# Reordering the ramp of a fused cross-attention and quantised FFN kernel

## Chip, cores and metric

The kernel runs on 1 core of a Trainium2 chip. The metric is device time in microseconds (us) of one execution. All times below come from one profiled execution of the kernel before, unless a median of runs is named.

## The reference

`x` is 4 x 2048 x 512 in fp32. It is first updated by an attention block and then by a feed-forward block.

```
attention: the mask leaves key j to query i only where j % 2048 == i; ctx has 154 rows
    row i < 154 : softmax over one unmasked key -> out row = ctx[i] @ Wv @ Wout + bout
    row i >= 154: all keys masked alike         -> out row = mean(ctx) @ Wv @ Wout + bout
x = x + out
h  = layernorm(layernorm(x)) * gamma + beta
hq = round(h * 127 / max|h|);  w1q = clip(round(w1 / mean|w1|), -1, 1)
g  = gelu(hq @ w1q.T * scales + b1)                      # 512 -> 2048
gq = round(g * 127 / max|g|);  w2q = clip(round(w2 / mean|w2|), -1, 1)
x  = x + gq @ w2q.T * scales + b2                        # 2048 -> 512
```

So the attention needs no softmax: it is the product Wv @ Wout applied to the context rows and to their mean, one set of rows for each of the 4 batches.

## The kernel before

The 8192 rows of x are cut into 64 tiles of 128 rows (`T`), rolled by two tiles, so that tiles 0 to 13 are rows of batch 0 which get only the mean row. Each engine runs one program whose order is written out by hand: SyncE (SP) issues loads, transposes and stores, ScalarE (ACT) and TensorE (PE), VectorE (DVE) and GpSimd (POOL) compute. Engines meet only through semaphores. A queue never steps past an instruction that waits.

**The ramp** (the lines ahead of the loops `for s in range(6, ...)`) does the work that happens once, beside the first six tiles:

- `context_mean` (L946, PE): the sum of the 154 rows of `ctx_b0` by a product with a tile of ones.
- `products` (L953, PE): Wv @ Wout, 32 fp32 products of 128x128 by 128x512, in 8 chunks `m` of the inner dimension (each waits for `wv` and `wout` of its chunk) and 4 quarters `k` of PSUM tile `p1`. It goes chunk by chunk, so all 4 quarters end together. Each product is two instructions of the trace.
- The mean row: DVE multiplies each chunk of Wv by the mean (`mean_product`, L669), ACT sums it (`mean_sum`, L497), DVE gathers (`mean_weighted`, L677), PE adds over partitions (`mean_row`, L963, after 14 of the 32 products), DVE adds the bias (`mean_row`, L688). POOL then adds this row to the tiles of x (`add_attention`, L323).
- w1 and w2: sum of absolute values (`abs_w1`, L503 and L728; `abs_w2`, L509), the total over partitions (`weight_total`, L967, PE, after 25 products), `weight_scale` (L740), rounding (`round_weights` L514, `round_w1` L747) and clipping (`clip`, L752).
- `copy_wvo` (L519, ACT) moves the product out of PSUM by quarters. `out_rows` (L974) and `tail_product` (L987) apply it to the context.
- b1: loaded four times over 32 partitions, split by POOL into three bf16 parts (`split_b1`, L316), and gathered by DVE into `b1rows` (`bias_rows`, L716).

**A tile t** passes: `add_attention` (POOL), `statistics` (DVE, L762), `inverse_std` (POOL, L337), `centre` (DVE, L768), `times_std` (ACT, L523), `add_beta` (POOL, L345), `x_scale` (DVE, L775), `round_x` (ACT, L528), `scale_rows` and `widen_x` (POOL, L357, L377), `transpose_x` (a DMA issued by SP, L214), `bias` (PE, L994) and `first_layer` (PE, L1007, two halves), `gelu` (ACT, L535, two halves), `half_scale`, `hidden_scale` (DVE, L787, L792), `round_h` (ACT, L544), `transpose_h` (DMA, L223), `widen_h` (DVE L803 and ACT L553, half each), `second_layer` (PE, L1017), `result` (DVE, L813), `store`. `bias(t)` writes over `p1`, so it waits for both `gelu` halves of tile t-1.

**Loads.** SP issues the context of batch 0, Wv, b1, w1 with x(1) to x(3) between, the context, x(4) to x(7). ACT issues Wout first, then x(0), bout, gamma, beta, then w2 in three goes; w2 pieces lie in buffers that other work frees (`load_w2_first` waits for `mean_done`, `load_w2_last` for `wvo_done`).

Of the kernel before, what the change touches and what calls it, by code (L numbers as in the profile page):

```python
# [33 lines left out]
def block_program(nc, x, ctxm_d, ctxt_d, wvT, wout_d, bout, w1T, b1, w2T, b2, gamma, beta, ctx_b0, out, tail_rows):  # L34
    es = ExitStack()
    with es:
# [6 lines left out]
        def sem(name):  # L43
# [55 lines left out]
        row_of = hT_words[:, P:P + 32]  # L99
        row_pick = hT_words[:, P + 32:P + 35]  # L100
        tail_out = wout[0:NB, 6, :]
        b1f = xq[:, :, :, :].rearrange("p a i n -> p (a i n)").bitcast(FP32)[:, 0:D]
        b1res = xqT[:, :, :, :, :].rearrange("p a i k n -> p (a i k n)").bitcast(FP32)[:, 0:2 * D]\
            .rearrange("p (a n) -> p a n", a=2)
        wv = hid[:, :, 0:HID].rearrange("p a (m n) -> p a m n", n=D)
        w2raw = [hqT[:, a, :, :, :].rearrange("p j e t -> p (j e t)").bitcast(FP32).rearrange("p (e n) -> p e n", e=2)
                 for a in range(2)]
        w2raw += [hq8[:, :, :].rearrange("p a n -> p (a n)").bitcast(FP32).rearrange("p (e n) -> p e n", e=2)]
        w2raw += [xr[:, 12:14, :], xr[:, 14:16, :]] + [wout[:, 2 * a:2 * a + 2, :] for a in range(3)]
# [13 lines left out]
        row_set, row_picked = sem("row_set"), sem("row_picked")  # L123
# [63 lines left out]
        def _(sp):  # L187
            def load_x(t):
                if t >= XS:
                    sp.wait_ge(y_stored[t % XS], 16 * (t // XS))  # L190
                sp.dma_start(xr[:, t % XS, :], x[t * P:(t + 1) * P, :]).then_inc(x_loaded[t % XS], 16)
# [4 lines left out]
            def load_w1(i):  # L196
                k, h = i // 2, i % 2
                sp.dma_start(raw1[:, k, h * HALF:(h + 1) * HALF], w1T[k * P:(k + 1) * P, h * HALF:(h + 1) * HALF])\
                    .then_inc(w1_loaded[i], 16)

# [30 lines left out]
            sp.dma_start(ctx_rows, ctx_b0[0:P, :]).then_inc(ctx_b0_loaded, 16)  # L231
            sp.dma_start(ctx_end, ctx_b0[P:KV, :]).then_inc(ctx_b0_loaded, 16)
            load_wv(0)
            for g in range(4):
                sp.dma_start(b1f[32 * g:32 * g + 32, :], b1[g * D:(g + 1) * D].partition_broadcast(32))\
                    .then_inc(b1_loaded, 16)
            for m in range(1, KI):
                load_wv(m)
            load_w1(0)
            load_w1(1)  # L240
            load_x(1)
            load_w1(2)
            load_x(2)
            load_w1(3)
            load_x(3)
            for i in range(4, 8):
                load_w1(i)
# [3 lines left out]
            for t in range(4, 8):  # L251
                load_x(t)
# [853 lines left out]
```

## Time and profile before

| | |
|---|---|
| median of 3 runs | 547.36 us (547.23 to 548.58) |
| time of the profiled execution | 546.68 us |
| its span (first to last instruction) | 545.0 us |
| busy: PE, DVE, ACT, POOL | 522.7, 451.2, 438.9, 404.7 us |
| idle time of PE in the span | 22.3 us |
| memory read, written | 34.08 MB, 17.00 MB |

The span is 1.7 us shorter than the time of its execution; the rest lies around the program. A busy time that stands near the span belongs to the engine that bounds the kernel on the average. Where in the span its idle time lies has to be read from the timeline.

### The profile page before, as it was taken

What the parts mean: (1) busy time and instruction counts of PE and PEld (TensorE: products, weight loads), DVE (VectorE), ACT (ScalarE), POOL (GpSimd) and SP (SyncE); (2) the same over time, 40 slices, a digit from 0 to 9 for tenths busy, and PEclk for the clock granted to TensorE, in tenths of its full rate; (3) what the DMA queues carried; (4) which work ended last, traced back from release to release, by engine and by line L of the source; (5) the groups of instructions that cost most, each with busy time, mean ns of one, the idle gap of its engine ahead of it and who ended that gap; (6) DMA issues with size and microseconds to landing.
All of it is one profiled execution on the core that took longest, in us unless ns stands there. A gap on an engine that the chain in (4) does not pass through costs nothing.

```text
span 545.0 us, 8050 instructions
## 1 busy us (share of the span) xinstructions
PE 522.7 (96%) x2371; PEld 224.9 (41%) x2418; DVE 451.2 (83%) x762; ACT 438.9 (81%) x444; POOL 404.7 (74%) x532
## 2 busy tenths in 40 slices
PE   6979887999999999999999999999999999999997
PEld 2433333444444444444444444444444444444443
DVE  1968998989998888888888888888888889887553
ACT  2557998968998888888888888888888888887762
POOL 2085795898998888888988888888888889873300
PEclk9988999999999999999999999999999999999999
DMA  9997226587554555455555555545555554434433
GB/s 285 397 395 227 90 43 156 114 232 179 137 140 128 121 127 134 129 141 140 133 126 125 120 141 139 126 123 121 122 139 132 140 141 102 99 67 102 101 78 97
DMA packets 136870, 78.88 MB, mean 145 GB/s; under 512 B 114037, under 2 KB 114037, under 8 KB 136827
## 3 DMA queue, kind: packets, MB, share of 16 engines
q1 hardware_dynamic: 133947, 71.03, 51.9%
q10 hardware_dynamic: 2880, 7.34, 3.8%
q8 instruction: 19, 0.31, 0.2%
q14 instruction: 24, 0.20, 0.1%
HBM read 34.08 MB, written 17.00 MB: 94 GB/s over the span
## 4 chain that ended last, share of the span: by engine, by line
PE 75%; issue 2%; ACT 2%; DMA 1%; SPq 1%; DVE 1%; POOL 0%; ACTq 0%; DVEq 0%; POOLq 0%
PE py L1028 37%; PE p L1013 36%; PE p L1003 3%; DMA hT<-hq 1%; DMA out<-xr 1%; ACT hid L541 1%; SPq L220 1%; ACT hq L550 0%; ACT hqT L559 0%; DVE xr L818 0%; SPq L228 0%; ACT xq L532 0%; DVE hmax L795 0%; DVE hid L789 0%; DVE xmax L777 0%
## 5 line engine op out<-in xcount | busy, mean ns | idle before, releaser
L1028 PE MATMUL py<-w2q,hqT 128*128 128x512 bf16 x1006 | 230.0, 379 | 3.8 <-DVE w2q L759 2.8
L1013 PE MATMUL p<-w1q,xqT 128*128 128x512 bf16 x995 | 229.0, 380 | 2.5 <-issue 1.4
L541 ACT ACTIVATE hid<-p,xdeq 128x1024 f32<-128x1024 f32 x128 | 141.7, 1108 | 26.8 <-PE p L1013 16.4
L550 ACT ACTIVATE hq<-hid,hscale 128x2048 int8<-128x2048 f32 x64 | 128.1, 2001 | 38.7 <-DVE hscale L801 38.7
L1028 PEld LDWEIGHTS py<-w2q,hqT 128*128 128x128 bf16 x1024 | 100.1, 98 | 123.9 <-issue 3.3
L1013 PEld LDWEIGHTS p<-w1q,xqT 128*128 128x128 bf16 x1024 | 95.0, 98 | 120.6 <-issue 14.9
L350 POOL TENSOR_TENSOR hx<-hx,beta_b 128x512 f32<-128x512 f32 x64 | 92.6, 1467 | 11.4 <-ACT hx L526 11.4
L795 DVE TENSOR_REDUCE hmax<-hid 128x1 f32<-128x1025 f32 x64 | 78.1, 1220 | 21.7 <-ACT hid L541 21.3
L335 POOL TENSOR_TENSOR xr<-xr,attn 128x512 f32<-128x512 f32 x64 | 81.8, 1295 | 18.0 <-DVE attn L691 13.3
L354 POOL TENSOR_TENSOR xr<-xr,b_b 128x512 f32<-128x512 f32 x64 | 92.4, 1462 | 0.0
L789 DVE TENSOR_REDUCE hid<-hid 128x1 f32<-128x1024 f32 x64 | 77.4, 1210 | 8.9 <-ACT hid L541 8.9
L809 DVE CAST hqT<-hT 128x1024 bf16<-128x1024 int8 x64 | 56.9, 889 | 27.7 <-PE py L1028 18.9
L559 ACT ACTIVATE hqT<-hT 128x1024 bf16<-128x1024 int8 x64 | 67.0, 1047 | 4.9 <-DMA hT<-hq 4.9
L381 POOL CAST xq<-xq 128x1024 bf16<-128x1024 int16 (+1 forms) x33 | 33.4, 1011 | 47.8 <-ACT xq L532 47.8
L772 DVE SCALAR_TENSOR_TENSOR hx<-xr,mv,gamma_b 128x512 f32<-128x512 f32 x64 | 53.4, 840 | 0.1
L818 DVE SCALAR_TENSOR_TENSOR xr<-py,hdeq,xr 128x512 f32<-128x512 f32 x64 | 47.4, 740 | 3.3 <-PE py L1028 3.3
L526 ACT ACTIVATE hx<-hx,rstd 128x512 f32<-128x512 f32 x64 | 42.8, 715 | 4.4 <-POOL rstd L342 2.6
L764 DVE BATCH_NORM_STATS2 stat<-xr 128x6 f32<-128x512 f32 x64 | 43.0, 672 | 0.6 <-POOL xr L335 0.6
L532 ACT ACTIVATE xq<-hx,xscale 128x512 int16<-128x512 f32 x64 | 42.7, 714 | 0.7 <-DVE xscale L784 0.7
L777 DVE TENSOR_REDUCE xmax<-hx 128x2 f32<-128x1024 f32 (+1 forms) x33 | 38.7, 1173 | 0.1
L385 POOL TENSOR_TENSOR hdeq<-hstep,wmean 128x1 f32<-128x1 f32 x64 | 25.5, 399 | 17.7 <-DVE hstep L798 17.7
L958 PE MATMUL p<-wout,hid 128*128 128x512 f32 x64 | 33.1, 679 | 0.0
(86 smaller groups left out, 290.9 us busy)
## 6 DMA issues: line engine op xcount, KB each, us to landing
out<-xr SPq DMA_DIRECT2D x64, 256.0 KB, 2.5
xr<-x SPq DMA_DIRECT2D x63, 256.0 KB, 2.9
raw<-w1T SPq DMA_DIRECT2D x8, 512.0 KB, 14.8
wout<-wout_d ACTq DMA_DIRECT2D x8, 256.0 KB, 7.1
hid<-wvT SPq DMA_DIRECT2D x8, 256.0 KB, 9.7
wout<-w2T ACTq DMA_DIRECT2D x3, 512.0 KB, 4.2
attn<-ctxm_d SPq DMA_DIRECT2D x4, 256.0 KB, 16.1
hqT<-w2T ACTq DMA_DIRECT2D x2, 512.0 KB, 7.8
```

Source lines behind the costliest of these rows:

```text
L335: pool.tensor_tensor(xtile(t, n), xtile(t, n), a, ALU.add).then_inc(x1_ready, n)
L350: pool.tensor_tensor(htile(t, n), htile(t, n), bb, ALU.add).then_inc(xnormed, n)
L354: pool.tensor_tensor(xtile(t), xtile(t), b2_b[:, :, :], ALU.add).then_inc(xb_ready, 1)
L541: nc.scalar.activation(hid[:, t % 2, h * HALF:(h + 1) * HALF], p1[:, h * HALF:(h + 1) * HALF], ACT.Gelu, scale=col(xdeq, t)).then_inc(gelu ...
L550: nc.scalar.activation(hq8[:, t % 2, :], hid[:, t % 2, 0:HID], ACT.Copy, scale=col(hscale, t))\
L559: nc.scalar.activation(hqT[:, t % 2, NJ // 2:, :, :], hT8[:, t % 2, HALF:].rearrange("p (j t e) -> p j e t", e=2, t=P), ACT.Copy).then_inc ...
L772: nc.vector.scalar_tensor_tensor(htile(t)[:, 0, :], xtile(t)[:, 0, :], mv[:, t % 8, 0:1], gamma_b[:, :], ALU.subtract, ALU.mult).then_inc( ...
L789: nc.vector.tensor_reduce(hid[:, t % 2, HID:HID + 1], hid[:, t % 2, 0:HALF], AX.X, ALU.max, apply_absolute_value=True).then_inc(hmax_half, 1)
L795: nc.vector.tensor_reduce(col(hmax, t), hid[:, t % 2, HALF:HID + 1], AX.X, ALU.max, apply_absolute_value=True).then_inc(hmax_done, 1)
L809: nc.vector.tensor_copy(hqT[:, t % 2, 0:NJ // 2, :, :], hT8[:, t % 2, 0:HALF].rearrange("p (j t e) -> p j e t", e=2, t=P))\
L1013: mm = nc.tensor.matmul(p1[:, n * D:(n + 1) * D], xT[:, k, :], w1q[:, k, n * D:(n + 1) * D], start=False, stop=(k == KD - 1))
L1028: mm = nc.tensor.matmul(py[:, t % 2, :], hqT[:, t % 2, c // 2, c % 2, :], w2q[:, c, :], start=(c == 0), stop=(c == 2 * NJ - 1))
```

## The change

Five things change, all of them in the ramp. The loops from tile 6 on stay as they are.

1. All loads but Wout go out on SP's queue, in a new order. w2 is issued by SP, two pieces ahead of the first `transpose_x` and six behind it. w2's pieces lie in other buffers. SP waits inside `load_x` for tiles 12 to 15.
2. `products` goes through quarters 0 and 1 of every chunk first, then through all chunks of quarter 2 and all of quarter 3. `weight_total(0)` stands after 30 products in place of 25. ACT's `copy_wvo` of each quarter is spread out between other work.
3. b1 is loaded once on 16 partitions, POOL splits it, SP stores the parts to memory and loads them back as `b1rows`. `bias_rows` of DVE and two selects of POOL go.
4. ACT starts with one small Gelu. PE starts with eight small products of ones by ones.
5. The written orders of SP, POOL, ACT, DVE and PE are rewritten. Among them: PE runs `out_rows` 1 and 2 ahead of the first layer of tile 0. POOL adds the mean row to four tiles ahead of the first `inverse_std`. `second_layer(0)` can begin on half of w2.

```diff
+            def load_w2(j):
+                if j == 3:
+                    sp.wait_ge(mean_done, 1)
+                if j == 5:
+                    sp.wait_ge(wvo_done, KD)
+                sp.dma_start(w2raw[j], w2T[j * 2 * P:(j + 1) * 2 * P, :].rearrange("(p e) n -> p e n", e=2))\
+                    .then_inc(w2_loaded[j], 16)
+            def store_b1():
+                sp.wait_ge(b1_split, 5)
...
+            def load_b1_rows():
+                sp.wait_ge(const_set, 4)
+                sp.wait_ge(b1_stored, 16)
+                for g in range(4):
+                    sp.dma_start(b1rows[32 * g:32 * g + 12, :], b1_pieces.rearrange("b a n -> (b a) n")[:, g * D:(g + 1) * D])\
+                        .then_inc(b1_rows, 16)
...
+            load_ctx_b0()
+            load_b1()
+            sp.dma_start(gamma_b[:, :], gamma.partition_broadcast(P)).then_inc(gamma_loaded, 16)
             load_wv(0)
...
+            load_wv(7)
+            load_x(0)
             load_w1(0)
             load_w1(1)
+            sp.dma_start(bout_b[:, :], bout.partition_broadcast(P)).then_inc(bout_loaded, 16)
             load_x(1)
+            load_x(2)
             load_w1(2)
             load_w1(3)
+            store_b1()
             load_x(3)
+            sp.dma_start(beta_b[:, :], beta.partition_broadcast(P)).then_inc(beta_loaded, 16)
+            load_w1(4)
+            load_w1(5)
+            load_x(4)
+            load_x(5)
+            load_x(6)
+            load_w1(6)
+            load_w1(7)
+            load_b1_rows()
+            load_w2(0)
+            load_ctx()
+            load_w2(1)
+            transpose_x(0)
+            load_w2(2)
...
+            load_w2(7)
+            load_x(7)
+            load_x(8)
+            load_x(9)
             sp.dma_start(b2_b[:, 0, :], b2.partition_broadcast(P)).then_inc(b2_loaded, 16)
+            load_x(10)
             transpose_x(1)
...
             pool.wait_ge(mean_copied, 1)
             add_attention(0, 1)
             add_attention(1, 1)
+            add_attention(2, 1)
+            add_attention(3, 1)
             pool.wait_ge(const_set, 3)
             inverse_std(0, 1)
+            inverse_std(1, 1)
...
+            def first_gelu():
+                act.wait_ge(const_set, 2)
+                nc.scalar.activation(wpart[:, 0, 6:8], neg_half[:, :], ACT.Gelu).then_inc(vmean_done, 1)
...
             abs_w1(1)
+            copy_wvo(0)
             abs_w1(2)
-            load_w2_first()
+            copy_wvo(1)
             abs_w1(3)
             times_std(0)
             abs_w1(5)
+            copy_wvo(2)
+            times_std(1)
             abs_w1(6)
             abs_w1(7)
-            times_std(1)
             round_x(0)
+            times_std(2)
+            times_std(3)
+            abs_w2(0)
+            copy_wvo(3)
             round_weights(0, 1)
             round_weights(0, 3)
...
+            def warm_up():
+                pe.wait_ge(const_set, 1)
+                for _ in range(8):
+                    nc.tensor.matmul(pa[:, 0:P], ones[:, :], ones[:, :], start=True, stop=True)
...
-                    m, k = i // KD, i % KD
-                    if k == 0:
+                    m, k = (i // 2, i % 2) if i < 2 * KI else (i % KI, i // KI)
+                    if i < 2 * KI and k == 0:
...
+            warm_up()
             context_mean()
             products(0, 14)
             mean_row()
-            products(14, 25)
+            products(14, 30)
             weight_total(0)
-            products(25, 32)
+            products(30, 32)
+            out_rows(0)
             bias(0)
-            out_rows(0)
+            out_rows(1)
+            out_rows(2)
             first_layer(0, 0)
             first_layer(0, 1)
-            out_rows(1)
-            tail_product()
             weight_total(1)
             bias(1)
             first_layer(1, 0)
             first_layer(1, 1)
-            out_rows(2)
+            out_rows(3)
             bias(2)
             first_layer(2, 0)
             first_layer(2, 1)
+            tail_product()
             bias(3)
             first_layer(3, 0)
             first_layer(3, 1)
-            out_rows(3)
             bias(4)
             first_layer(4, 0)
-            second_layer(0)
             first_layer(4, 1)
+            second_layer(0, 0, NJ)
+            second_layer(0, NJ)
             second_layer(1)
             bias(5)
             first_layer(5, 0)
+            second_layer(2)
             first_layer(5, 1)
-            second_layer(2)
```

In the cut parts ACT's new order goes on: `abs_w2(1)`, `times_std` 4 and 5, `round_x(1)`, `abs_w2` 2, 4, 3, 5, 6, 7, then the Gelu of tile 0 with `round_x` 2 and 3. DVE's new order between the scale of w1 and its rounding is: statistics(5), x_scale(1), three `ctx_sum`, centre(5), x_scale(2,2), `attn_rows(0)`, the fourth `ctx_sum`, `round_w1` 0 and 2, four clips, `attn_rows` 1 and 2, `weight_sum(1)`.

## Rows read from the trace of the kernel before

**Rows 1.** Timeline of PE: start, duration, line, operands, count, idle before and releaser.
```profile
5.31 2.04 PE L949 MATMUL py<-hx,hT 128*128 128x512 f32 x2 [5.31 <-DMA hx<-ctx_b]
...
9.28 14.17 PE L958 MATMUL p<-wout,hid 128*128 128x512 f32 x28
23.75 1.12 PE L965 MATMUL py<-xr,hT 128*128 128x512 f32 x2 [0.29 <-DVE xr L685]
24.71 9.61 PE L958 MATMUL p<-wout,hid 128*128 128x512 f32 x22
37.30 0.56 PE L970 MATMUL py<-wsum,hT 128*128 128x1 f32 x2 [2.98 <-DVE wsum L738]
37.72 9.29 PE L958 MATMUL p<-wout,hid 128*128 128x512 f32 x14
47.79 0.40 PE L1003 MATMUL p<-b1rows,xqT 32*128 32x512 bf16 x4 [0.78 <-ACT wvo L521]
48.11 3.70 PE L983 MATMUL pa<-wvo,attn 128*128 128x512 f32 x8
51.87 3.40 PE L1013 MATMUL p<-w1q,xqT 128*128 128x512 bf16 x15
```

**Rows 2.** The same view from 60 us to the end of the ramp.
```profile
63.56 0.35 PE L970 MATMUL py<-wsum,hT 128*128 128x1 f32 x2 [1.42 <-DVE wsum L738]
...
76.66 0.40 PE L1003 MATMUL p<-b1rows,xqT 32*128 32x512 bf16 x4 [1.54 <-ACT hid L541]
...
89.04 3.61 PE L1028 MATMUL py<-w2q,hqT 128*128 128x512 bf16 x16 [2.83 <-DVE w2q L759]
...
105.11 0.40 PE L1003 MATMUL p<-b1rows,xqT 32*128 32x512 bf16 x4
```

**Rows 3.** What PE waited for after 135 us: total, times, longest.
```profile
PE p L1013 <- issue: 1.3, 8, 0.2
```

**Rows 4.** Stretches: length, busy of PE, PEld, DVE, ACT, POOL (instructions), granted clock, DMA share, GB/s.
```profile
30.00:40.00 10.00, 7.02 (x16) 3.17 (x15) 6.74 (x16) 6.51 (x10) 8.62 (x11) 0.85 1.04 392
40.00:50.00 10.00, 9.22 (x21) 3.56 (x20) 7.25 (x12) 6.90 (x9) 4.27 (x8) 0.81 0.86 248
50.00:60.00 10.00, 9.95 (x32) 4.46 (x32) 9.74 (x18) 9.97 (x18) 8.23 (x12) 1.00 0.44 142
...
140.00:300.00 160.00, 158.89 (x772) 68.66 (x786) 141.06 (x243) 137.49 (x133) 138.87 (x177) 1.00 0.55 132
```

**Rows 5.** Timeline of ACT.
```profile
30.36 0.72 ACT L526 ACTIVATE hx<-hx,rstd 128x512 f32<-128x512 f32 x1 [2.60 <-POOL rstd L342]
...
35.73 1.06 ACT L506 ACTIVATE w1q<-raw 128x1024 bf16<-128x1024 f32 x1 [1.42 <-DMA raw<-w1T]
...
38.16 0.72 ACT L532 ACTIVATE xq<-hx,xscale 128x512 int16<-128x512 f32 x1 [0.67 <-DVE xscale L784]
...
44.47 0.60 ACT L521 ACTIVATE wvo<-p 128x512 f32<-128x512 f32 x1 [1.80 <-PE p L958]
...
57.40 1.28 ACT L541 ACT_TABLE_LOAD   x1
...
87.19 1.06 ACT L559 ACTIVATE hqT<-hT 128x1024 bf16<-128x1024 int8 x1 [2.63 <-DMA hT<-hq]
...
105.56 2.00 ACT L550 ACTIVATE hq<-hid,hscale 128x2048 int8<-128x2048 f32 x1
```

**Rows 6.** Timeline of DVE.
```profile
19.68 0.69 DVE L674 TENSOR_TENSOR hx<-hid,hx 128x512 f32<-128x512 f32 x1 [0.54 <-DMA hid<-wvT]
20.29 3.40 DVE L685 SCALAR_TENSOR_TENSOR xr<-wout,attn,xr 128x512 f32<-128x512 f32 x4
...
44.90 3.35 DVE L749 TENSOR_SCALAR w1q<-raw,wscale 128x2048 int16<-128x2048 f32 x2
48.17 3.56 DVE L759 TENSOR_SCALAR w1q<-w1q 128x2048 bf16<-128x2048 int16 x4
```

**Rows 7.** Timeline of POOL.
```profile
26.55 2.50 POOL L335 TENSOR_TENSOR xr<-xr,attn 128x512 f32<-128x512 f32 x2 [13.32 <-DVE attn L691]
```

**Rows 8.** Timeline of SP's queue.
```profile
41.58 15.98 SPq L220 DMA_TRANSPOSE xqT<-xq  x2
```

More of the change, by code:

```diff
@@ L31, with block_program @@
 QMAX = 127.0
-def block_program(nc, x, ctxm_d, ctxt_d, wvT, wout_d, bout, w1T, b1, w2T, b2, gamma, beta, ctx_b0, out, tail_rows):
+def block_program(nc, x, ctxm_d, ctxt_d, wvT, wout_d, bout, w1T, b1, w2T, b2, gamma, beta, ctx_b0, out, tail_rows, b1_pieces):
     es = ExitStack()
@@ L255, in _ @@
             transpose_x(1)
-            for t in range(8, 12):
-                load_x(t)
+            load_x(11)
+            load_x(12)
+            load_x(13)
             transpose_x(2)
@@ L269, in _ @@
             sp.dma_start(tail_rows, tail_out).then_inc(tail_stored, 16)
+            store(0)
+            transpose_x(6)
+            transpose_x(7)
             transpose_h(3)
-            transpose_x(6)
+            load_x(16)
             transpose_h(4)
@@ L848, in _ @@
             statistics(1)
+            statistics(2)
+            statistics(3)
             abs_w1(4)
             centre(1)
-            statistics(2)
-            statistics(3)
+            centre(2)
+            x_scale(0, 1)
+            centre(3)
+            statistics(4)
             weight_sum(0)
-            x_scale(0, 1)
+            centre(4)
             weight_scale(0)
-            centre(2)
-            centre(3)
+            statistics(5)
+            x_scale(1, 1)
             ctx_sum(0)
             ctx_sum(1)
-            x_scale(1, 1)
+            ctx_sum(2)
+            centre(5)
+            x_scale(2, 2)
+            attn_rows(0)
+            ctx_sum(3)
             round_w1(0)
@@ L866, in _ @@
             clip(0, 3)
-            ctx_sum(2)
-            ctx_sum(3)
-            statistics(4)
-            attn_rows(0)
-            centre(4)
-            statistics(5)
+            attn_rows(1)
+            attn_rows(2)
+            weight_sum(1)
             ctx_means()
+            weight_scale(1)
+            x_scale(4, 2)
+            half_scale(0)
             statistics(6)
-            x_scale(2, 2)
-            centre(5)
-            centre(6)
             statistics(7)
-            weight_sum(1)
@@ L894, in _ @@
-            statistics(11)
+            tail_rows_out()
+            statistics(11)
+            hidden_scale(2)
+            clip(1, 0)
+            clip(1, 1)
+            clip(1, 2)
+            clip(1, 3)
+            clip(1, 4)
+            clip(1, 5)
+            widen_h(0)
+            widen_h(1)
+            clip(1, 6)
+            clip(1, 7)
+            half_scale(3)
+            x_scale(6, 2)
+            centre(9)
+            result(0)
+            half_scale(4)
+            widen_h(2)
@@ L1015, in first_layer, with second_layer @@
                 mm.then_inc(ffn1_done, 1)
-            def second_layer(t):
+            def second_layer(t, first=0, last=2 * NJ):
                 pe.wait_ge(hcast_dve, t + 1)
```

300 lines of the change are left out of this document (119 added, 181 removed).

## The prediction

> **What bounds the kernel now.** I read the busy shares first: PE is busy 96% of the span, the other three 74 to 83%. The stretches then split the span in two. From 140 to 300 us PE is busy 158.9 of 160 us [rows 4], and after 135 us it waits for nothing but 1.3 us of issue [rows 3]. The loops are bound by PE, the diff leaves them as they are, and the tail with them. So everything from `bias(6)` at 105.11 us to the end of the span, 439.9 us, is taken as fixed, and the question is when `bias(6)` starts.
>
> The timeline of PE says what lies ahead of it. Idle: 5.31 us before the first load has landed, 0.29 before the mean row, 2.98 before the total of w1, 0.78 before `bias(0)` [rows 1], then 1.42 before the total of w2, 1.54 before `bias(3)`, 2.83 before `second_layer(0)` [rows 2]. Together 15.2 us. The rest is TensorE at its lower level. 22 product instructions take 9.61 us, 0.437 each; behind the wait of 2.98 us 14 of them take 9.29, where 6.1 would do: 3.2 us lost [rows 1]. There the granted clock averages 0.85 and 0.81 against 1.00 elsewhere, part of the time at 1.2 in place of 2.4 GHz [rows 4]. The start is slow too: four instructions from 5.31 to 9.28 us are 0.99 us each, and 28 more take 14.17 us where 12.2 would do; that is 2.2 and 1.9 us [rows 1]. All in all some 22.5 us are lost of 105.1, and PE's work in the ramp is about 82.6 us. No order can bring `bias(6)` below 82.6 plus the first landing.
>
> The other engines set how much of that can be had. From 50 to 60 us DVE is busy 9.74 and ACT 9.97 of 10 us [rows 4]: past 50 us the ramp is bound by the work of ACT and DVE, not by PE. PE's gaps at 63, 76 and 89 us are their lateness seen from PE.
>
> **Part by part.**
>
> *Warm start.* Eight small products of ones begin at about 1 us, when the tile of ones is set, where PE is idle. At 0.99 us for 512 columns an instruction of 128 columns is about 0.25 us, so 16 of them last about 4 us, up to the landing at 5.31: they cost nothing. PE then has some 4 us of activity behind it. The 1.9 us lost in the first 28 product instructions are four or so at twice the duration, so before the shorter ones begin around 12 us; with TensorE active 4.3 us sooner I put that at about 8. I take 3 us as gained, between 0 (the small products don't count) and 4.1.
>
> *What is late next.* With that and chunk 0 landed, the products start at about 8.5 us and are at the mean row after 14 x 0.87, at 20.7. The mean row needs the last chunk of Wv. It lands at 19.68 before, and four weighted sums behind it end at 23.69 [rows 6]. x(0), bout, gamma and beta no longer share the bandwidth from ACT's queue, against which gamma is now ahead of Wv: about 0.5 MB fewer at 392 GB/s [rows 4], 1.3 us. So the mean row runs at about 22.4, PE has waited 1.7 us for it, and the mean row is 1.4 us earlier than 23.75 [rows 1]: more than half of the warm start is given back here. From 23.3 the other 18 products last 15.7 us, to 39.0. Before they end at 47.0.
>
> *The total of w1.* In front of it stand 16 products now and 11 before, so PE reaches it at about 37 us. Its releaser is the last `abs_w1`, at 35.73, which waits 1.42 us for its load [rows 5]. Bytes ahead of the last w1 piece fall: the w2 pieces that ACT issues meanwhile are behind it now, while x(4) to x(6) are ahead. Net it lands 1 to 2 us earlier, so the sum is there at about 36. The wait of 2.98 us and the 3.2 us of slow clock behind it go: 6.2 us.
>
> *TensorE's clock once more.* In this trace the wait of 2.98 us is followed by 1.2 GHz, while those of 1.42, 1.54 and 2.83 us are not [rows 1, 2]. The new wait of about 1.7 us is nearer to those. The Trainium skill ("TensorE: Matmul & The Clock Gate", "The HAM clock gate") says that the throttled level is the default and that activity releases it. The slow first products agree with it, though the granted clock shown there is 1.00.
>
> *First layer of tile 0.* It doesn't move, and this is the step that I find easiest to overlook. It needs w1 rounded and clipped. The chain is: four `add_attention` of 1.25 us on POOL [rows 7] in place of two ahead of `inverse_std(0)`, which eats the mean row's 1.4 us; ACT waits 2.60 us at 30.36 for that very result [rows 5], so `round_x(0)` comes at about 36, not 38.16; the scale of w1 comes at about 37.5 us, not 38.3. Then DVE has about 7 us of statistics, `ctx_sum`, `x_scale` and `attn_rows(0)` before `round_w1` (3.3 us) and four clips (3.5 us) [rows 6]; the first clip ends at about 50, and PE, behind three `out_rows` of 3.6 us [rows 1], begins the first layer at 51.2 against 51.87. What is gained is what is already done by then: two `out_rows`, 7.2 us. PE is 7.9 us ahead, `copy_wvo` is done, and the bottleneck is ACT.
>
> *ACT, the sum.* ACT's loop starts at 105.56 us, and its `round_x(0)` begins at 38.16 [rows 5]. In these 67.4 us it idles 6.4 us: 1.80 before `copy_wvo`, 2.63 before `widen_h(0)` [rows 5], and 2.0 us in six small gaps. The new order has the same work, less three `copy_wvo` of 0.6 us, done earlier (1.8 us), less the second table load, 1.28 us, done at the start. It starts 1.4 to 2 us earlier. Of the 6.4 us of idle I leave 2.5: walking the written order with these durations ACT still stands about 1 us before the first Gelu of tile 3 and 1 us before the last of tile 5, for PE. Sum: 1.8 + 1.3 + 1.6 + 3.9 = 8.6 us earlier. For the Gelu the Trainium skill ("ScalarE: Activation LUTs", "What ACT_TABLE_LOAD costs") gives about 2.7 us with a drain, where the trace has 1.28; by the page the sum would be 1.4 us larger.
>
> *PE and the rest of the walk.* On PE the same walk gives: `bias(1)` at 56, `bias(2)` at 63.6 behind `out_rows(3)`, `bias(3)` at 71, `bias(4)` at 76, `second_layer(0)` at 79.6, `second_layer(1)` at 83, `bias(6)` at 94.9. That is 10.2 us ahead of 105.11, more than ACT's 8.6, because `second_layer(2)` now fills a wait. From tile 6 on both run in step, so ACT's figure decides. DVE loses 2.1 us of `bias_rows`. All else is the same work on DVE and POOL, and they arrive with ACT.
>
> *b1.* The store and the loads back are 5 DMAs for 4, and behind them on SP wait w2(0), the context and `transpose_x(0)`. `load_b1_rows` waits for a store which is queued behind about 7.5 MB, so it lands near 26 us. Some 3 MB are still queued then, 7 us of cover. Cost 0. Without the cover it would be the store's round trip, for which the rows have no price: between 0 and the 15.98 us that two transposes and what lay between them held the queue [rows 8]. I take 0.
>
> *w2 behind `transpose_x(0)`.* Six pieces, 3.1 MB, at 392 GB/s last 8 us [rows 4]. The transpose is issued at about 40.4 us (before at 41.58 [rows 8]), so the last piece lands at 51.7, and `abs_w2(7)` starts at 52.2. Cost 0, cover 0.5 us. `transpose_x(1)` is queued behind these and four tiles of x and lands near 55.5, with `bias(1)` at 56. Cover again 0.5 us.
>
> The sum is 8.6 us. Span 545.0 - 8.6 = 536.4. With the 1.7 us around it: **538.0 us**. The profiled execution, 546.68, lies 0.7 us below the median of 547.36; by the median it would be 538.7. Both lie well inside the range.
>
> **Rivals.**
>
> 1. *PE alone bounds the ramp.* ACT and DVE keep up. Then `bias(6)` comes at 5.3 + 82.6 + 1.7 + 2 us of small waits = 91.6: 13.5 us, time 533. For it: the other engines' idle time before 38 us. Against: they have hardly any from 50 us on [rows 4].
> 2. *The clock falls again and the loads are late.* The wait for the mean row grows towards 3 us, as one that the lower level followed [rows 1]: 3.2 us of slower products, `copy_wvo(2)`, which stands in ACT's order ahead of two `abs_w1` and `round_x(0)`, is 2 to 3 us later, and all of ACT's 8.6 with it. With 1 to 2 us from w2 landing late, 4 us remain: 542.5. The row of 2.83 us that no fall followed [rows 2] speaks against a sure one.
> 3. *Slower: one in-order queue couples the tiles and the weights.* SP holds six of eight w2 pieces until tile 0 is rounded and widened. Every us by which `transpose_x(0)` is late is a us on `abs_w2(7)`, the total of w2, the rounding of w2, and `second_layer(0)`. It decides from about 41 us on and turns the gain into a loss at 41 + 8.6 = 49.6 us. Two falls of the clock ahead of quarter 2 of the product (2 x 3.2 us) plus a late x(3) could do it. For 3 us more the time is 550. Against: before, that transpose went out at 41.58 with a worse start of PE.
> 4. *The change does nothing.* What ACT gains before 50 us is spent in waits of DVE and POOL (`widen_x(2)` waits for a later `round_x(3)`): within 0.3%, 547.
>
> **How the numbers follow.** Forecast (536 to 541) 0.5; rival 1 (532 to 536) 0.18; rival 2 (541 to 545) 0.19; rival 4, 0.06; rival 3, 0.07. Faster by more than 0.3% (1.6 us, about what a measurement of this kernel can tell) is the first three: 0.87. The range from 533.0 to 543.5 leaves out the lower end of rival 1, the upper third of rival 2 and both others, 0.2 together. It holds the unknown costs taken at 0 up to 5.5 us.
>
> **What would show it.** Right: no wait at the total of w1 and clock 1.00 from 30 to 50 us; products done near 39; first layer of tile 0 still near 51; one table load; `bias(6)` at 95 to 98; the same 440 us after it. Wrong: a wait of more than 1 us for w2 in ACT near 50 us (rival 3), a granted clock of 0.5 after the mean row (rival 2), PE without waits from 50 to 95 us (rival 1), or a span from `bias(6)` on that is longer than 440 us, which would say that the loops inherit a backlog that I have not priced.

## The result and the profile after

The changed kernel runs in 543.13 us (median of 6 runs, 541.95 to 544.97), the kernel before in 547.36 us (median of 5, 546.10 to 548.58). Two executions in a slow state, one of 3097.6 us of the kernel before and one of 916.95 us of the run with two additions first, are left out of all medians and ratios. The ratio is 0.9915, interval 0.9896 to 0.9935: 0.85% faster, clear of noise, and half of the 1.7% forecast. The time lies just inside the range; the direction was right, the size was not.

| | before | after | forecast |
|---|---|---|---|
| time of the profiled execution | 546.68 | 543.86 | 538.0 |
| its span | 545.0 | 542.0 | 536.4 |
| first product on PE | 9.28 | 11.17 | 8.5 |
| mean row on PE | 23.75 | 25.37 | 22.4 |
| first layer of tile 0 | 51.87 | 54.88 | 51.2 |
| `bias(1)` | 63.8 | 61.04 | 56 |
| `bias(6)` | 105.11 | 100.86 | 94.9 on PE's walk, 96.5 by ACT's 8.6 us |
| `round_h(5)`, where ACT's loop starts | 105.56 | 104.46 | 97.0 |

The spans differ by only 3.0 us where the medians differ by 4.2, since the profiled execution of before lies 0.7 us below its median and that of after 0.7 us above its own.

The timeline of PE of the changed kernel, as in [rows 1] and [rows 2] (start, duration, line, operands, count, idle before and releaser):

```profile
0.97 3.79 PE L964 MATMUL pa<-hT 128*128 128x128 f32 x16 [0.97 <-POOL rr L356]
4.90 1.21 PE L970 MATMUL py<-hx,hT 128*128 128x512 f32 x2
6.04 1.12 PE L971 MATMUL py<-hx,hT 26*128 26x512 f32 x2
11.17 14.36 PE L979 MATMUL p<-wout,hid 128*128 128x512 f32 x28 [4.00 <-DMA hid<-wvT]
25.37 1.02 PE L986 MATMUL py<-xr,hT 128*128 128x512 f32 x2
26.23 13.90 PE L979 MATMUL p<-wout,hid 128*128 128x512 f32 x32
40.38 0.35 PE L991 MATMUL py<-wsum,hT 128*128 128x1 f32 x2 [0.26 <-DVE wsum L754]
...
54.88 0.81 PE L1034 MATMUL p<-w1q,xqT 128*128 128x512 bf16 x3 [0.54 <-DVE w1q L775]
...
61.04 0.39 PE L1024 MATMUL p<-b1rows,xqT 32*128 32x512 bf16 x4 [1.80 <-DMA xqT<-xq]
...
100.86 0.40 PE L1024 MATMUL p<-b1rows,xqT 32*128 32x512 bf16 x4 [1.72 <-ACT hid L574]
101.19 3.63 PE L1034 MATMUL p<-w1q,xqT 128*128 128x512 bf16 x15
105.81 3.63 PE L1049 MATMUL py<-w2q,hqT 128*128 128x512 bf16 x16 [1.00 <-DVE hqT L825]
```

The warm-up does what it says: `context_mean` takes 2.3 us in place of 4.0. Then PE idles **4.00 us** for chunk 0 of Wv, a wait that the kernel before doesn't have, and the 28 product instructions behind it again take 14.36 us, not 12.2. The wait at the total of w1 is gone, 2.98 to 0.26 us.

The stretches of the changed kernel, with the columns of [rows 4], show where TensorE's lower level now lies: from 10 to 20 us, at 0.73, and no longer from 30 to 50 us.

```profile
0.00:10.00 10.00, 6.05 (x20) 4.20 (x20) 0.69 (x1) 1.49 (x2) 3.48 (x13) 0.93 0.64 225
10.00:20.00 10.00, 8.83 (x16) 3.94 (x17) 6.60 (x11) 4.18 (x12) 0.00 (x0) 0.73 1.05 397
...
30.00:40.00 10.00, 10.00 (x24) 4.18 (x22) 9.14 (x16) 6.24 (x13) 9.43 (x11) 1.00 0.97 348
40.00:50.00 10.00, 9.05 (x26) 3.80 (x26) 8.83 (x21) 9.52 (x13) 9.32 (x18) 1.00 0.43 141
```

And single microseconds of the changed kernel at the head of the loads (length, granted clock, DMA share, GB/s):

```profile
3.00:4.00 1.00, 1.00 1.06 404
4.00:5.00 1.00, 1.00 1.07 297
5.00:6.00 1.00, 1.00 0.47 137
6.00:7.00 1.00, 1.00 0.46 174
7.00:8.00 1.00, 1.00 0.75 258
```

From 5 to 7 us the DMA engines are half idle and move 137 and 174 GB/s. That is where the broadcast of gamma stands in the queue, ahead of Wv. The second profile of this kernel (r_after) has 125 and 197 GB/s there at shares of 0.69 and 0.63: the low rate repeats, the share less so. This gave the theory of the first experiments: what is missing was lost before the first product.

### The profile page after: what moved, and what is told of

Same layout as the page of the kernel before. It is cut to its first block, busy times and chain, and to the rows that moved or that the text cites. A ratio compares the mean times of both kernels' runs of the same rounds, so it can differ in the third digit from the quotient of the medians.

```text
span 542.0 us, 8082 instructions
## 1 busy us (share of the span) xinstructions
PE 521.8 (96%) x2387; PEld 226.6 (42%) x2434; DVE 452.4 (83%) x758; ACT 436.8 (81%) x444; POOL 408.4 (75%) x533
## 4 chain that ended last, share of the span: by engine, by line
PE 77%; DVE 3%; issue 2%; ACT 1%; DMA 1%; DVEq 0%; ACTq 0%
PE py L1049 37%; PE p L1034 36%; PE p L1024 3%; DVE hmax L811 1%; DMA hT<-hq 1%; DVE hx L788 1%; DVE hid L805 0%; ACT hid L574 0%; ACT hq L583 0%; DVE xr L834 0%; DVE stat L780 0%; DVE xmax L793 0%; ACT hqT L592 0%; DVE hqT L825 0%; DVE hstep L814 0%
## 5 line engine op out<-in xcount | busy, mean ns | idle before, releaser
L385 POOL TENSOR_TENSOR xr<-xr,attn 128x512 f32<-128x512 f32 x64 | 83.3, 1321 | 19.1 <-DVE attn L723 19.1
L825 DVE CAST hqT<-hT 128x1024 bf16<-128x1024 int8 x64 | 58.5, 917 | 25.0 <-PE py L1049 17.4
L431 POOL CAST xq<-xq 128x1024 bf16<-128x1024 int16 (+1 forms) x33 | 34.8, 1055 | 47.8 <-ACT xq L565 47.8
L788 DVE SCALAR_TENSOR_TENSOR hx<-xr,mv,gamma_b 128x512 f32<-128x512 f32 x64 | 55.4, 870 | 0.1
L435 POOL TENSOR_TENSOR hdeq<-hstep,wmean 128x1 f32<-128x1 f32 x64 | 23.9, 376 | 17.7 <-DVE hstep L814 17.7
L979 PE MATMUL p<-wout,hid 128*128 128x512 f32 x64 | 30.2, 630 | 4.0 <-DMA hid<-wvT 4.0
```

What stands on the lines that cost most here:

```text
L385: pool.tensor_tensor(xtile(t, n), xtile(t, n), a, ALU.add).then_inc(x1_ready, n)
L788: nc.vector.scalar_tensor_tensor(htile(t)[:, 0, :], xtile(t)[:, 0, :], mv[:, t % 8, 0:1], gamma_b[:, :], ALU.subtract, ALU.mult).then_inc( ...
L825: nc.vector.tensor_copy(hqT[:, t % 2, 0:NJ // 2, :, :], hT8[:, t % 2, 0:HALF].rearrange("p (j t e) -> p j e t", e=2, t=P))\
```

## The experiments

Each median is of 4 to 12 executions. The ratio is always to the kernel before, measured beside them; its medians there were 548.06 us (r_after, e1, e2, e3), 549.10 (e4, e5, e6, e9), 547.38 (e7, e8, e10) and 547.94 (e11), so medians of different sets are compared with care. The last column is the start of ACT's loop.

| run | median us | ratio (interval) | first product | mean row | `bias(6)` | `round_h(5)` |
|---|---|---|---|---|---|---|
| changed kernel again (r_after) | 542.14 | 0.9888 (0.9856 to 0.9921) | 11.35 | 26.12 | 101.16 | 103.08 |
| gamma behind Wv (e1_gamma_late) | 538.84 | 0.9818 (0.9788 to 0.9848) | 7.47 | 21.04 | 96.64 | 100.25 |
| no warm-up (e2_no_warm) | 542.07 | 0.9877 (0.9844 to 0.9910) | 10.89 | 25.32 | 100.54 | 102.47 |
| gamma and bout ahead of Wv (e3_two_first) | 543.60 | 0.9912 (0.9882 to 0.9943) | 12.41 | 26.62 | 104.08 | 106.01 |
| x(0) ahead of Wv, gamma behind (e9_x0_ahead) | 540.34 | 0.9839 (0.9806 to 0.9871) | 9.17 | 24.32 | 99.66 | 101.58 |
| gamma ahead, wait filled (e11_filled_gap) | 540.52 | 0.9861 (0.9840 to 0.9883) | 10.88 | 24.20 | 99.22 | 101.15 |
| gamma behind, no warm-up (e5_gamma_late_no_warm) | 539.91 | 0.9838 (0.9808 to 0.9869) | 8.95 | 23.15 | 98.15 | 100.08 |
| gamma behind, transpose_x(1) first (e4_late_xt1) | 538.96 | 0.9814 (0.9784 to 0.9844) | 8.21 | 21.82 | 98.88 | 100.80 |
| gamma behind, two additions first (e8_two_adds) | 539.34 | 0.9829 (0.9793 to 0.9865) | 7.97 | 21.38 | 98.42 | 100.35 |
| gamma behind, widen_h(3) early (e10_widen3) | 538.94 | 0.9839 (0.9805 to 0.9873) | 7.96 | 21.73 | 97.05 | 101.26 |
| before, total of w1 late (e6_total_late) | 547.44 | 0.9979 (0.9952 to 1.0006) | 9.03 | 24.09 | 104.92 | 105.37 |
| before, warm-up alone (e7_warm_alone) | 550.27 | 1.0038 (1.0015 to 1.0061) | 7.77 | 25.76 | 110.25 | 110.70 |

**The changed kernel again.**

> The changed kernel once more, as the base for the edits beside it. In its first profile chunk 0 of Wv was there at 11.15 us, PE idled 4.0 us before its first product, bias(1) waited 1.8 us for its transpose and bias(6) began at 100.9 us. Expected by all theories: 0.9915 of the kernel before, within 0.2%, the same wait of 4 us and the same start of bias(6), within 1 us.

Its ratio is 0.27% below the one expected, a little more than allowed for, and the two intervals overlap; its wait for chunk 0 is 3.72 us and its `bias(6)` 0.3 us later, while ACT's loop starts 1.4 us earlier. Differences of under 1.5 us between medians are not relied on below.

**gamma behind Wv.**

```
             load_ctx_b0()
             load_b1()
-            sp.dma_start(gamma_b[:, :], gamma.partition_broadcast(P)).then_inc(gamma_loaded, 16)
             load_wv(0)
...
             load_wv(7)
+            sp.dma_start(gamma_b[:, :], gamma.partition_broadcast(P)).then_inc(gamma_loaded, 16)
             load_x(0)
```

> The broadcast of gamma is issued behind the last chunk of Wv instead of ahead of the first. Theory A (the missing gain was lost at the head of SP's queue: gamma's 0.26 MB broadcast arrives at about half rate and holds chunk 0 back): chunk 0 is there at 8.7 to 9.3 us instead of 11.15, the wait of 4.0 us shrinks to about 2, the slow clock from 10 to 17 us goes, the mean row moves from 25.4 to about 23, and bias(6) from 100.9 to 98 to 99; 2 to 3 us faster than the changed kernel. Rival B (the ramp is bound past 50 us by DVE, POOL and ACT, whatever the start): the mean row moves, bias(6) doesn't by more than 0.5 us. Rival C (the bandwidth, not the order: moving gamma only moves who waits): the last chunk of Wv lands when it did and the mean row moves by less than 0.5 us.

538.84 us, 3.3 below the changed kernel beside it and 0.8 from the 538.0 forecast. The two sets of six executions don't overlap (537.41 to 539.95 against 541.39 to 544.52). Timeline of PE of this run:

```profile
7.47 12.28 PE L979 MATMUL p<-wout,hid 128*128 128x512 f32 x28 [0.35 <-DMA hid<-wvT]
21.04 1.13 PE L986 MATMUL py<-xr,hT 128*128 128x512 f32 x2 [1.28 <-DVE xr L717]
...
56.82 0.40 PE L1024 MATMUL p<-b1rows,xqT 32*128 32x512 bf16 x4 [1.79 <-DMA xqT<-xq]
...
96.64 0.40 PE L1024 MATMUL p<-b1rows,xqT 32*128 32x512 bf16 x4 [1.73 <-ACT hid L574]
```

The wait is 0.35 us, the 28 instructions take 12.28 us, which is the full clock, and the mean row now waits 1.28 us for DVE, as the prediction had said it would. From there everything is 4.2 to 4.3 us earlier than in the changed kernel: `bias(1)` 56.82 against 61.04, `bias(6)` 96.64 against 100.86. Theory A holds in kind, and all its sizes were too small (first product at 8.7 to 9.3, mean row at 23, 2 to 3 us). B, that the later ramp would swallow it, falls, and so does C, that only the bandwidth counts: the mean row moved by 4.3 us. The rate of the loads at the same place, with the columns as above:

```profile
5.00:6.00 1.00, 1.00 0.97 330
6.00:7.00 1.00, 1.00 1.00 342
7.00:8.00 1.00, 1.00 0.99 371
```

**No warm-up.** The call of `warm_up()` is left out.

> The changed kernel without the eight small products of ones. Theory A: the wait of 4 us for chunk 0 makes TensorE fall back to 1.2 GHz anyway, so the warm-up only shortens context_mean (from about 3.9 to 2.2 us, hidden in that wait) and is worth nothing: within 0.1% of the changed kernel, mean row within 0.5 us. Rival: it is worth the 3 us that I had put down for it, and without it the mean row moves to 27 or later and the time grows by 1 to 3 us.

542.07 against 542.14 us: nothing, as theory A says. PE waits 2.05 us instead of 3.72, starts the products at the lower level either way, and the mean row is at 25.32, 0.8 us earlier than with the warm-up where 0.5 was allowed for; 0.46 of it is an earlier first product.

**Two broadcasts ahead of Wv.** The load of bout moves to the place behind gamma's, ahead of `load_wv(0)`.

> A dose of the suspected cost: the broadcast of bout goes ahead of Wv too, behind gamma's. Theory A: a second broadcast of 0.26 MB delays chunk 0 by the same 1.5 to 2.3 us again, to about 13 us, the mean row to about 27.2, and bias(6) by 1.5 to 2 us; 1.5 to 2 us slower than the changed kernel. Rival B (start doesn't count): same time as the changed kernel. Rival D (bytes only: 0.26 MB at 400 GB/s): chunk 0 later by 0.7 us.

1.5 us slower than the changed kernel in the median, with overlapping intervals. The first product moves by 1.06 us (11.35 to 12.41), between D's 0.7 and A's 1.5 to 2.3, and the mean row by 0.5. So the second broadcast costs less than the first. The dose has the right sign but not A's size. The profiled execution lost more, 2.9 us at `bias(6)`. Of that 1.7 us is the first layer of tile 1, which ran in part at TensorE's lower level behind the wait for its transpose (granted clock 0.72 from 63 to 69 us):

```profile
63.00 0.39 PE L1024 MATMUL p<-b1rows,xqT 32*128 32x512 bf16 x4 [2.10 <-DMA xqT<-xq]
63.33 5.31 PE L1034 MATMUL p<-w1q,xqT 128*128 128x512 bf16 x16
```

The same 5.31 us stand behind a wait of 2.05 us in the run with `transpose_x(1)` first and of 2.06 us with two additions first; in the others it takes 3.6 us.

**x(0) in gamma's place.** gamma and x(0) change places.

```
-            sp.dma_start(gamma_b[:, :], gamma.partition_broadcast(P)).then_inc(gamma_loaded, 16)
+            load_x(0)
             load_wv(0)
...
             load_wv(7)
-            load_x(0)
+            sp.dma_start(gamma_b[:, :], gamma.partition_broadcast(P)).then_inc(gamma_loaded, 16)
```

> In the changed kernel x(0) and gamma change places: x(0), as large as the gamma broadcast but 128 different rows, stands ahead of Wv. It tells why gamma hurts. Theory A1 (a row broadcast to 128 partitions moves at about half the rate of a plain load at the head of the queue): chunk 0 comes about 0.7 us later than in e1_gamma_late, so near 8.2 us, against 11.2 with gamma there; bias(6) near 97.5; about 0.7 us slower than e1_gamma_late. Theory A2 (it is the bytes ahead of chunk 0, of whatever kind, and the wait that they make): chunk 0 near 11 us, a wait of 4 us, 1.2 GHz behind it, and the time of the changed kernel.

Neither size is met. The same 0.26 MB as plain rows put the first product at 9.17, 1.7 us behind gamma late (7.47) and 2.2 ahead of gamma first (11.35). A1's 0.7 us was too little. So of gamma's 3.9 us about 1.7 come with a plain load of that size there, and 2.2 with its being this broadcast. These are single executions: the first product of the four kernels with gamma late and the warm-up lies between 7.47 and 8.21, that of the three with gamma alone ahead of Wv and no filled wait between 10.89 and 11.35. What slows the broadcast stays open. x(0) there is followed by the lower level too:

```profile
9.17 15.31 PE L979 MATMUL p<-wout,hid 128*128 128x512 f32 x28 [2.00 <-DMA hid<-wvT]
```

**The wait filled.** In the changed kernel, gamma still first, 16 more small products of ones stand behind `context_mean`.

```
             warm_up()
             context_mean()
+            warm_up()
+            warm_up()
             products(0, 14)
```

> The changed kernel with gamma where it put it (ahead of Wv), and 16 more small products of ones behind context_mean, some 3.6 us, so that TensorE is active while it waits for chunk 0. It splits what gamma's place costs into lateness and clock. Theory A: the wait of 4 us shrinks to under 1, the first products run at 2.4 GHz, and the 28 instructions ahead of the mean row take 12.3 us in place of 14.4; chunk 0 is as late as before, so the mean row moves from 25.4 (26.1) to 23.5 to 24, and the time lies about half way between the changed kernel and e1_gamma_late: 1.5 to 2 us faster than the changed kernel. Rival: the clock is nothing and lateness all; the time is that of the changed kernel.

```profile
7.21 3.84 PE L964 MATMUL pa<-hT 128*128 128x128 f32 x32
10.88 12.24 PE L979 MATMUL p<-wout,hid 128*128 128x512 f32 x28
24.20 1.12 PE L986 MATMUL py<-xr,hT 128*128 128x512 f32 x2 [1.07 <-DVE xr L717]
```

Chunk 0 is nearly as late as before (DVE takes it at 10.82, 11.32 in r_after), but the 28 instructions take 12.24 us and the time is 540.52, half way between 542.14 and 538.84. So gamma's place cost 3.3 us, part by the clock and part by lateness: 1.6 and 1.7 by the medians, 1.5 and 2.4 by the ratios, 1.9 and 0.9 by the start of ACT's loop. That both parts are there is shown: the four executions (540.36 to 540.62) lie between the ranges of the other two kernels. How they divide isn't settled, since this run was timed in another set and the intervals of its ratio overlap both others. The clock isn't worth its full 2.1 us because the mean row then waits 1.07 us for DVE.

**gamma behind Wv, no warm-up.**

> gamma behind Wv as in e1_gamma_late, and no small products of ones at the start. Theory A (the warm-up pays only if no gap of several us follows it): here it has something to pay for: without it context_mean takes 4 us, the first products run at the lower level, the mean row moves from 21.0 to 23 to 24 us and the time grows by 2 to 3 us over e1_gamma_late, while in e2_no_warm it cost nothing. Rival: the warm-up is worth nothing here either, within 0.5 us of e1_gamma_late, and what e1_gamma_late gained came from the earlier chunk alone.

1.1 us slower than with the warm-up (ratios 0.9838 and 0.9818, intervals overlapping), the mean row 2.1 and `bias(6)` 1.5 us later, ACT's loop 0.2 us earlier. The mean row moved as theory A says; of the time only half of the 2 to 3 us came, and by the medians alone it is not settled whether the warm-up is worth 1 us here or nothing.

**gamma behind Wv, `transpose_x(1)` ahead of five loads.** It moves from behind `load_x(10)` to behind `load_w2(7)`.

> gamma behind Wv as in e1_gamma_late, and transpose_x(1) issued ahead of the loads of x(7) to x(10) and b2 instead of behind them. Theory A (in-order coupling of transposes and loads on one queue, named in rival 3 of the prediction, costs its wait one for one): in e1_gamma_late bias(1) waits 1.79 us for this transpose; with 1.3 MB less ahead of it the transpose lands 2 to 3 us earlier, the wait goes and bias(6) moves from 96.6 to about 95: 1 to 1.8 us faster than e1_gamma_late. Rival B (bias(1) has just missed its Gelu anyway, and ACT's queue sets the pace): bias(1) moves, but later waits for the Gelu grow by as much and bias(6) stays within 0.5 us.

```profile
57.80 0.40 PE L1024 MATMUL p<-b1rows,xqT 32*128 32x512 bf16 x4 [2.05 <-ACT hid L574]
```

The wait for the transpose is gone and a wait of 2.05 us for the Gelu of tile 0 stands in its place. 538.96 against 538.84 us, and ACT's loop 0.55 us later: rival B, not the 1 to 1.8 us of A. B's other sign, `bias(6)` within 0.5 us, failed: it is 2.2 us later, of which 1.7 us are the first layer of tile 1 at the lower level (0.66 from 58 to 63 us). The coupling on the queue is real, but here only one of two things that end together.

**gamma behind Wv, two additions ahead of `inverse_std(0)`.** POOL's order is that of before at this place.

> e1_gamma_late with POOL's order as in the kernel before at this place: two add_attention, inverse_std(0), then two more, then inverse_std(1). Theory A: ACT's wait of 3.2 us for the first rstd goes, but the scale of w1 stays where it is, behind TensorE's 30th product near 36 us, and so do transpose_x(0) and the rest: within 0.5 us of e1_gamma_late. Rival (the prediction's sentence that the four additions eat what the mean row gained): round_x(0), the total of w1 and transpose_x(0) all move up by 1 to 2.5 us and the time falls by 1 to 2 us.

539.34 against 538.84 us: no gain, and ACT's loop starts at 100.35 and 100.25. ACT's first wait shrinks and the next one takes it up. Timeline of ACT, first of gamma late, then of this run:

```profile
29.44 0.72 ACT L559 ACTIVATE hx<-hx,rstd 128x512 f32<-128x512 f32 x1 [3.23 <-POOL rstd L392]
```

```profile
27.22 0.72 ACT L559 ACTIVATE hx<-hx,rstd 128x512 f32<-128x512 f32 x1 [0.66 <-POOL rstd L392]
...
31.13 0.60 ACT L554 ACTIVATE wvo<-p 128x512 f32<-128x512 f32 x1 [1.91 <-PE p L979]
```

`copy_wvo(2)` stands at 31.1 us in both, close behind TensorE's 24th product. `round_x(0)` doesn't come earlier (34.92 and 35.16). The prediction's sentence that the four additions eat the gain of the mean row is wrong as a cause: TensorE's place in the product decides. (`bias(6)` is 1.8 us later in this profile, 1.7 of it the first layer of tile 1 named above.)

**gamma behind Wv, `widen_h(3)` early on DVE.** It moves ahead of `x_scale(8, 2)` and `hidden_scale(5)`.

> e1_gamma_late with DVE's half of widen_h(3) moved up, ahead of x_scale(8,2) and hidden_scale(5). In e1_gamma_late second_layer(3) waits 1.0 us for it just behind bias(6). Theory A: that wait goes, and as ACT reaches the Gelu of tile 6 no sooner (round_h(5) waits for hidden_scale(5), now 0.6 to 1 us later), bias(7) stays where it is or moves back: within 0.5 us of e1_gamma_late either way. Rival: the 1.0 us comes through to the end.

538.94 us: nothing. Timeline of PE of this run:

```profile
106.36 0.40 PE L1024 MATMUL p<-b1rows,xqT 32*128 32x512 bf16 x4 [1.90 <-ACT hid L574]
106.69 5.31 PE L1034 MATMUL p<-w1q,xqT 128*128 128x512 bf16 x16
```

The wait of 1.0 us before `second_layer(3)` has gone, `bias(7)` waits 1.90 us for the Gelu, and the first layer behind it runs in part at the lower level, 5.31 us for 3.63. The wait that was taken away isn't in every execution, as shown below.

**The kernel before with the total of w1 late.** `weight_total(0)` after 30 products instead of 25, nothing else.

> The kernel before with one part of the change: weight_total(0) stands after 30 products of 32, not after 25. The prediction gave this part 6.2 us on TensorE (a wait of 2.98 and 3.2 of lower clock). Theory A: the wait and the lower clock go, the product ends near 41 instead of 47.0 us, but w1's scale comes at 40.5 instead of 38.3, and past 50 us ACT and DVE bound the ramp; as their start is set by copy_wvo and the scale, 2 to 4 us come through at bias(6). Rival: 6 us come through, since copy_wvo and out_rows are all 6 us earlier. Other rival: nothing, since the rounding of w1 is later by as much as the product is earlier.

```profile
38.78 0.28 PE L970 MATMUL py<-wsum,hT 128*128 128x1 f32 x2
38.92 1.96 PE L958 MATMUL p<-wout,hid 128*128 128x512 f32 x4
46.53 0.61 PE L1003 MATMUL p<-b1rows,xqT 32*128 32x512 bf16 x4 [5.65 <-DMA xqT<-xq]
```

The product ends at 40.9 us instead of 47.0 [rows 1], and then TensorE waits 5.65 us for the transpose of tile 0. The product is 6.1 us earlier. 4.9 of it goes in that wait (it was 0.78), and 2.6 in the `out_rows(0)` behind it, which takes 6.30 us in place of 3.70, at a granted clock of 0.50 from 46 to 52 us. The first layer of tile 0 so starts at 53.21, 1.3 us later than before. `bias(6)` comes 0.2 us earlier, and the ratio's interval holds 1: the outcome of the third theory, but not by its cause, since ACT's rounding of w1 starts only 0.7 us later (39.49 against 38.79). TensorE's loss there had been hidden behind the transpose. Whether the part is worth something with the loads and tile orders of the rest of the change no run shows.

**The kernel before with the warm-up alone.**

> The kernel before with one part of the change alone: eight small products of ones ahead of context_mean. The prediction took 3 us for it. Theory A: context_mean and the first products get short, the mean row can't come much before 22.5 us as it waits for the last chunk of Wv, and the wait for the total of w1 (2.98 us) grows by what TensorE is earlier, because that is set by the loads of w1: nothing comes through, within 0.2% of the kernel before. Rival: 2 to 3 us faster than the kernel before.

```profile
25.76 2.08 PE L970 MATMUL py<-xr,hT 128*128 128x512 f32 x2 [4.67 <-DVE xr L685]
27.63 10.15 PE L963 MATMUL p<-wout,hid 128*128 128x512 f32 x22
```

Neither theory: 0.38% **slower** (interval 1.0015 to 1.0061). The first 14 products end early, the mean row waits 4.67 us for the last chunks of Wv, and behind that wait TensorE is at its lower level: the mean row's own product takes 2.08 us instead of 1.12. It also starts 2.0 us later than in [rows 1], since the last chunk of Wv lands 2.0 us later than in [rows 6]. Timeline of DVE of this run:

```profile
21.70 0.69 DVE L674 TENSOR_TENSOR hx<-hid,hx 128x512 f32<-128x512 f32 x1 [0.65 <-DMA hid<-wvT]
22.31 3.40 DVE L685 SCALAR_TENSOR_TENSOR xr<-wout,attn,xr 128x512 f32<-128x512 f32 x4
```

Why the loads were later when only TensorE's program changed stays open; the earlier mean row that the warm-up should have allowed could not come. At `bias(6)` (110.25) the kernel is 5.1 us late; 2.7 of these come in one place, where the lower level follows a wait again (granted clock 0.50 from 92 to 96 us). Timeline of PE:

```profile
91.48 6.32 PE L1033 MATMUL py<-w2q,hqT 128*128 128x512 bf16 x16 [3.37 <-DVE w2q L759]
```

It took 3.61 us in [rows 2]. This profiled execution, 552.02 us, is the longest of the run, 1.75 us above its median.

## Why the prediction was half right

**Where it failed.** The step is *What is late next*: "With that and chunk 0 landed, the products start at about 8.5 us". It takes the landing of chunk 0 for granted, and it names gamma ahead of Wv only as bytes in a sum. [rows 1] gave no landing for chunk 0: the first product began at 9.28 behind `context_mean`, so chunk 0 was only known to be there by then, and the 8.5 had no row of its own. Measured: 11.17, with a wait of 4.00 us and the lower level behind it. The mean row came at 25.37 and not at 22.4, 3.0 us late. With gamma behind Wv it came at 21.04 and the time was 538.84. So this one term cost 3.3 us by the medians; the filled wait shows clock and lateness in it.

The same step has a second number that was off. "About 0.5 MB fewer" ahead of the last chunk of Wv is short of the trace: x(0), bout and beta are 0.26 MB each, and the four loads of b1, which stood between chunks 0 and 1 on SP's queue before, are 0.26 MB together: 1.05 MB in all. Yet DVE's last four weighted sums end at 24.45 in the changed kernel, where the prediction had 22.4 and before had 23.69; with gamma behind Wv they end at 20.98. So in these profiles gamma's place delays the whole of Wv by about 3.5 us, against the 0.7 us of its bytes.

**The second step that failed** is in *ACT, the sum*: "Of the 6.4 us of idle I leave 2.5". ACT's loop was to start 8.6 us earlier, at 97. It starts at 104.46 (103.08 in the second profile). `round_x(0)` is at 39.15 (39.90) and not at 36, which is the late start above. From there to its loop ACT idles 7.1 us (5.0), not 2.5 (the 6.4 of before are 7.1 too by the trace): 1.87 for w2, 1.8 for PE, 2.9 for `hidden_scale`. With gamma late it still idles 7.0 us, and its loop starts at 100.25, 3.3 us behind 97.

**Luck.** The time of the version with gamma late, 0.8 us from the forecast, therefore doesn't vindicate the sum. Two errors cancel in its span of 537.8: ACT's loop 3.3 us late, and the stretch behind it 1.9 us shorter than was taken as fixed (below, at the fixed 439.9 us).

**Warm start.** "I take 3 us as gained", between 0 and 4.1: in the changed kernel 0, the lower end, as the run without it shows. With gamma late it moves the mean row by 2.1 us, and the time by 1.1 at most. The small products raise the clock: the second context product takes 1.12 us here, where it took 2.07 before. The rule of the Trainium skill ("TensorE: Matmul & The Clock Gate", "The HAM clock gate") that activity releases the throttle agrees with it; the granted clock of 0.73 from 10 to 20 us shows that the release didn't last through the wait.

**The total of w1.** Right as to TensorE: the wait went from 2.98 to 0.26 us and the granted clock from 30 to 50 us is 1.00, though at 40.38 and not at about 37. Wrong as a gain by itself: alone it gave nothing.

**First layer of tile 0.** "It doesn't move": right only with gamma late, 50.66 against 51.2 forecast; in the changed kernel it moved back 3.0 us to 54.88, with two more `out_rows` done ahead of it as said. The four clips took 4.64 us, not 3.56 [rows 6], with waits of 0.5 and 0.6 us at PE for them.

**The walk after it.** With gamma late it reads 56.8, 64.1, 71.5, 76.7, 80.5 for `bias(1)` to `bias(4)` and `second_layer(0)`, against 56, 63.6, 71, 76 and 79.6. `bias(6)` came at 96.64, against 94.9: 1.7 us short, and next to the 96.5 of ACT's sum. ACT reads as follows in the changed kernel:

```profile
52.77 1.06 ACT L544 ACTIVATE w2q<-hqT 128x1024 bf16<-128x1024 f32 x1 [1.87 <-DMA hqT<-w2T]
...
94.62 2.00 ACT L583 ACTIVATE hq<-hid,hscale 128x2048 int8<-128x2048 f32 x1 [1.35 <-DVE hscale L817]
...
104.46 2.00 ACT L583 ACTIVATE hq<-hid,hscale 128x2048 int8<-128x2048 f32 x1 [1.58 <-DVE hscale L817]
```

And in its second profile (r_after):

```profile
93.97 2.00 ACT L583 ACTIVATE hq<-hid,hscale 128x2048 int8<-128x2048 f32 x1 [0.16 <-DVE hscale L817]
...
103.08 1.99 ACT L583 ACTIVATE hq<-hid,hscale 128x2048 int8<-128x2048 f32 x1
```

"All else is the same work on DVE and POOL, and they arrive with ACT" was wrong from about 90 us on in the first: there ACT waits 2.9 us for DVE's `hidden_scale`. In the second it waits 0.16 us. The difference begins at DVE's `widen_h(2)`, which waits 1.05 us for its transpose at 91.61 us in the first and not at all in the second; of the other profiles only those of gamma late (1.02) and of `widen_h(3)` early (1.10) have that wait. It comes with the execution: the second profile is 0.7 us behind the first at `bias(1)` and ends 1.4 us ahead of it. The loads of w2 behind `transpose_x(0)` cost 1.87 us of wait in ACT (1.72 in the second profile) where I had 0 with a cover of 0.5; this was the sign named for rival 3.

**ACT's table.** Right: one load, at 5.98 us, and none later. No run splits its share from the rest.

**b1.** Right: SP waited 2.5 us for the store, under cover.

**The fixed 439.9 us.** From `bias(6)` to the end it takes 441.1, with new waits of 1.0 us before `second_layer(3)` and 0.2 before `bias(8)`. That looks like the sign named for an inherited backlog, but in the second profile both waits are missing and the stretch takes 439.4; only the three executions with the late transpose have more than 440.1. `bias(6)` was the wrong mark. From the start of ACT's loop to the end of the span it takes 437.5 us in both profiles of the changed kernel and in seven of the nine kernels built on it (438.0 with gamma behind and no warm-up, 438.9 with `widen_h(3)` early), and 439.4 to 439.6 in the kernel before and its two variants. So the orders of the change are worth 1.9 us behind the ramp, which the prediction took as fixed; through what, no run shows.

**Rivals.** Rival 2 had 542.5 us by a wait on TensorE, 1.2 GHz behind it, and late products. That is nearly the time and the mechanism, but it stood before the mean row in my text and was before the first product on the chip. Rival 3, in-order coupling, shows as the wait of 1.80 us at `bias(1)` and of 1.87 us for w2 in ACT; taking the first away gave nothing, the second wasn't tried. Rivals 1 and 4 fell.

The version with gamma behind Wv is faster than both kernels: 0.9818 of the kernel before.

## What to carry to other kernels

The first transfers of a queue can cost more than their bytes, 3.9 us at the first product here for 0.26 MB: put a small or broadcast operand that is needed late behind the first operand that TensorE needs, and read the first landing in the profile before pricing anything that comes after it. A TensorE brought to its upper level has to be kept busy until its real work is there; with a wait of 4.0 us in between the warm-up bought nothing here. Where several queues arrive together, taking away one wait mostly uncovers the next, so price a part only after finding what is late next on each engine. And take the fixed stretch from the engine that sets the pace there, and from more than one profile: here `bias(6)` and ACT's loop start moved by different amounts.

## What the runs showed of the hardware

Unexpected was the rate of the broadcast at the head of the queue: 137 and 174 GB/s at DMA shares of 0.47 and 0.46 from 5 to 7 us, where the same stretch without it had 330 and 342 at 0.97 and 1.00, and with the plain load of x(0) in its place 344 and 375 at 0.98 and 0.99. In the second profile of the changed kernel it was 125 and 197 at 0.69 and 0.63. It cost 2.2 us more than the plain transfer of the same size; a second one behind it cost only 1.1. SP needed 6.06 us to issue the eight loads of Wv behind it, and 4.33 us behind x(0).

The length of a wait alone doesn't tell whether TensorE's clock falls behind it. 1.2 GHz followed a wait of 1.12 us in the run with `widen_h(3)` early (first row below) and not the longer one of 2.83 us in [rows 2]; the run with two additions first, without a wait there, stayed at 2.4 GHz (second row). Nor does a length found in one place hold in another: at `bias(1)` the clock fell behind waits of 2.05, 2.06 and 2.10 us and not behind 2.03 (x(0) ahead of Wv), while at `bias(7)` it fell behind 1.90 (`widen_h(3)` early). The columns are length, busy time of PE, granted clock, DMA share and GB/s.

```profile
8.00:12.00 4.00, 4.00 (x6) 0.59 1.05 403
```

```profile
8.00:12.00 4.00, 4.00 (x10) 1.00 1.06 403
```
